# A wait for landed gathers in the middle of each group of the two max passes

## The reference

```
def _gin_layer(h, src, dst, W, b):
    msgs = h[src]
    agg = jax.ops.segment_max(msgs, dst, num_segments=N_NODES)
    agg = jnp.where(jnp.isfinite(agg), agg, jnp.zeros_like(agg))
    return (h + agg) @ W + b
x = _gin_layer(h, src, dst, W1, b1)
x = jax.nn.relu(x)
x = _gin_layer(x, src, dst, W2, b2)
```

## Time and profile before

| | |
|---|---|
| median of 3 timed runs | 5820.93 us (5820.36 to 5821.15) |
| span of the one profiled execution | 6562.2 us |
| POOL busy in that span | 3944.3 us, 60% |
| DVE busy | 4507.3 us, 69% |
| PE busy | 2310.6 us, 35% |

### The profile page before, as it was taken

The page is one execution under the profiler, slowest core; times in us unless marked ns, Lnnn a source line. Parts: engine busy times, 40 slices in busy tenths (PEclk is TensorE's granted clock), DMA queues, the critical chain, the costliest instruction groups (busy, mean ns, idle before and its releaser), DMA issues.

```text
span 6562.2 us, 44574 instructions
## 1 busy us (share of the span) xinstructions
PE 2310.6 (35%) x14635; PEld 1387.8 (21%) x14635; DVE 4507.3 (69%) x5353; ACT 2519.0 (38%) x3136; POOL 3944.3 (60%) x3878
## 2 busy tenths in 40 slices
PE   4988400000020000000100000046877783778886
PEld 2775300000000000000000000023444441444443
DVE  7978587777767777776787777764655653656654
ACT  2330144444424444443344444433444442444443
POOL 1001377777747777775677777656665555566664
PEclk8998755555555555555555555567888895889887
DMA  2233354444434444443454444412333322333332
GB/s 64 83 136 135 110 163 152 153 147 146 152 117 151 157 148 147 152 148 113 134 160 152 147 148 146 142 46 86 102 110 101 101 95 73 102 110 109 98 103 84
DMA packets 257146, 807.72 MB, mean 123 GB/s; under 512 B 72026, under 2 KB 108938, under 8 KB 253123
## 3 DMA queue, kind: packets, MB, share of 16 engines
q0 software_dynamic: 162688, 416.67, 22.2%
q1 hardware_dynamic: 94279, 389.14, 16.2%
HBM read 473.23 MB, written 332.30 MB: 123 GB/s over the span
## 4 chain that ended last, share of the span: by engine, by line
POOL 38%; PE 26%; issue 22%; DVE 8%; ACT 2%; another core or an unknown queue 2%; DMA 1%; SPq 0%; DVEq 0%; POOLq 0%; ACTq 0%
POOL arena L2316 38%; PE pair_ps L1864 20%; PE pair_ps L1966 3%; DVE outs L917 2%; ACT outs L1702 1%; PE banks_ps L1830 1%; PE banks_ps L1942 1%; DVE outs L995 1%; PE pair_ps L1873 0%; DVE bn_st L700 0%; DVE H L1048 0%; ACT arena L1680 0%; PE pair_ps L1982 0%; PE banks_ps L1807 0%
## 5 line engine op out<-in xcount | busy, mean ns | idle before, releaser
L2316 POOL DMA_INDIRECT arena<-table,src_i x3596 | 3684.6, 1025 | 1549.8 <-issue 1134.4
L1842 PE MATMUL pair_ps<-ident,tails 128*128 128x128 f32 x9 | 2.7, 439 | 3331.7 <-DVE tails L1246 3331.7
L1864 PE MATMUL pair_ps<-bias,arena 128*128 128x384 bf16 x4050 | 803.9, 348 | 279.9 <-issue 239.9
L1092 DVE TENSOR_TENSOR pair_ps<-pair_ps,arena 128x1792 f32<-128x1792 f32 x168 | 341.5, 2033 | 764.7 <-DMA arena<-table,src_i 589.1
L1864 PE MATMUL pair_ps<-work,arena 128*128 128x384 bf16 x4050 | 760.5, 338 | 206.4 <-issue 204.8
L995 DVE TENSOR_TENSOR_SCAN outs<-arena,banks_ps 128x1920 f32<-128x1920 f32 x112 | 465.2, 4153 | 494.3 <-ACT banks_ps L1688 446.2
L1842 PEld LDWEIGHTS pair_ps<-ident,tails 128*128 128x128 f32 x9 | 1.5, 213 | 3334.0 <-DVE tails L1246 3334.0
L1140 DVE TENSOR_TENSOR_SCAN work<-work,banks_ps 128x1920 f32<-128x1920 f32 x168 | 697.7, 4153 | 5.8
L1562 ACT ACTIVATE LD<-DE 128x112 f32<-128x112 f32 x168 | 49.8, 296 | 1440.9 <-issue 571.3
L1864 PEld LDWEIGHTS pair_ps<-bias,arena 128*128 128x128 bf16 x4050 | 406.9, 102 | 661.6 <-issue 452.8
L1582 ACT COPY outs<-work 128x1792 f32<-128x1792 f32 x171 | 541.0, 3165 | 0.0
(11 more groups left out here) (321 smaller groups left out, 4353.4 us busy)
## 6 DMA issues: line engine op xcount, KB each, us to landing
rows_att<-outs SPq DMA_DIRECT2D x165, 1008.0 KB
rows_plain<-outs SPq DMA_DIRECT2D x110, 896.0 KB
arena<-table,src_i POOLq DMA_INDIRECT x3596
kept_counts<-arena SPq DMA_DIRECT2D x15, 2000.0 KB, 6.4
bias<-sources SPq DMA_DIRECT2D x108, 192.0 KB
arena<-kept_counts SPq DMA_DIRECT2D x10, 2000.0 KB, 8.3
outs<-kept_counts SPq DMA_DIRECT2D x5, 2000.0 KB, 8.0
table<-arena SPq DMA_DIRECT2D x18, 512.0 KB, 3.0
```

The source lines that it names most:

```text
L1092: chain(v.tensor_tensor(prod, prod, ring[:, s, :, 0:D], ALU.mult))
L1864: ins = pe.matmul(picked_ps[g % 2], parts3[:, a, t, :], hots_made[g % 2][:, :, t, :], start=t == a == 0, stop=t == NB - 1 and a == 2)
L2316: pool.indirect_dma_start(dst, None, tab, bass.IndirectOffsetOnAxis(ap=idx, axis=0))\
```

## The change

In both max passes POOL gets one more wait in each group: after the first half of the group's gathers (7 of 14 in groups 0 and 1, 5 of 11 after them) it waits until all of that half have landed, and only then issues the second half. That is 56 waits in a pass and 112 in all. No instruction is moved, added or removed on the other engines, and the attention passes are as they were.

```diff
                         if g >= RING:
                             pool.wait_ge(s_spread, scanned(k, g - RING))
-                        for j in range(GROUP - picks(k, g)):
+                        n = GROUP - picks(k, g)
+                        for j in range(n):
+                            if j == n // 2:
+                                pool.wait_ge(s_land[g % RING], landed(k, g) - 16 * (n - j))
                             fetch(ring_plain[:, g % RING, j, :], table[k], src_i[:, g * GROUP + j:g * GROUP + j + 1],
                                   s_land[g % RING])
```

## The result

| | before | after |
|---|---|---|
| median of the timed runs | 5820.65 us (5817.55 to 5821.15, 4 runs) | 5992.16 us (5987.11 to 6000.26, 4 runs) |
| span of the recorded execution | 6562.2 us first, 5811.0 us when it was recorded again | 5992.8 us |
| idle time before the edge gathers (L2316, 3596 of them), ended by a gather's landing | none | 208.1 us |

The ratio is 1.0297 with a 95% interval of 1.0282 to 1.0311: 171.5 us slower, 171.5 / 112 = 1.53 us for each of the 112 waits. Forecast were 5980 us and 1.41 us.

The account below looks back on a forecast made before the run. POOL was taken to bound the timed max passes, 13.0 us a group against PE's 12.5; 112 waits x 1.41 us = 158 us on 5821 gave 5979, rounded to 5980 us, own range 5920 to 6045, overall range 5815 to 6100.

Parts of the forecast that it names:

- POOL ends last in the timed max passes: In the timed max passes POOL needs 13.0 us a group against PE's 12.5 us, so it has no slack.
- The split of the 741 us: Profiled execution's excess over the timed median: 403 us from PE's idle time in max passes, 338 us from 3745 gathers.
- The price of a wait: On POOL in the max passes: 2.60 us from gather to waiter's start, less 1.185 us, so 1.41 us a wait.
- two neighbours in the trace: Two trace places used to price a wait: ACT waiting for a group 0 gather, and POOL waiting for its own scatter.
- The scatter's 1.24 us: Where POOL waits for its own scatter to HBM, idle is 1.54 instead of 0.30 us; would make 139 us in all.
- All 112 waits count: In both max passes each wait passes straight to ACT, DVE's scan and the next slot: 112 x 1.41 = 158 us.
- The span: Profiled execution's span, 6562.2 us, would move by under 30 us, POOL's 3.6 us of slack a group covering the waits.
- The test I gave: If the recorded span moves as much as the timed median, both have the same bound and the 741 us reading is wrong.
- No change: Rival, chance 0.18: PE's idle time is in timed max passes too, waits vanish in the ring of slots; 5827 us.
- faster: Rival, chance 0.13: pauses in mid-group let PE run in the max passes, saving 146 us; 5675 us.
- PE's stall: In profiled max passes PE idles 1.6 to 2.3 us between matmuls of one group, without releaser; taken as absent when timed.
- Much slower: Rival, chance 0.09: in half the max-pass groups DVE's compares hold the gather after the pause, adding 308 us; 6287 us.

Follow-up runs that it names:

- four kernels of the table: Four edits of the kernel before: one wait mid-group (the change), after the 3rd gather (6013.7 us) or after the 7th (6039.2 us), and two waits a group (6311.4 us).
- The kernel with eight gathers: Kernel before with 8 gathers instead of 11 in each group from the third on: 5644.0 us; with the change's waits besides, 5653.3 us.
- the kernel with two waits: The change with two waits a group, after a third and two thirds of the gathers, instead of one in the middle: 6311.4 us, ratio 1.0836 to the kernel before.
- the late wait: The change with its one wait after the 7th gather of every group instead of the middle: 6039.2 us, ratio 1.0393 to the kernel before.

## Why the prediction was right

**POOL ends last in the timed max passes.** Right, and it carried the forecast. The profile that I had showed the opposite, 3.6 us of slack in every group. What turned it was the 741 us between the first recording and the median, and that PE's idle time had no releaser and stood inside a group. The second recording shows it: no such idle time, no slack of POOL. The margin over PE is larger than forecast, 14.0 against 12.5 us and not half a microsecond. Had I read the slack straight, I would have forecast no change.

**The split of the 741 us.** Half right. The prediction put 403 us of them in the max passes and took the other 338 us from the gap before every gather, so that a timed gather would come every 1.185 us and a group take 13.0 us. It comes every 1.27 us, and a group takes 14.0 us: the gap of 0.30 us before a gather is real. What was slow in the first recording's attention passes was the gathers themselves, 1056 ns; in the second:

```profile
L2316 POOL DMA_INDIRECT arena<-table,src_i x603 | 578.3, 959 | 183.7 <-issue 182.2 <-DVE pair_ps L1085 1.5
```

603 gathers in the 800 us that held 570. From the first edge gather to the last, the two max passes took 1004.0 and 993.1 us in the first recording and 790.2 and 790.1 us in the second, 417 us less, close to the 403 forecast; the three attention passes took 244.5 us less, and the rest of the 751 us between the two spans lies outside these passes. The wrong step was to spread the other 338 us over the gap before every gather. The error was harmless for the forecast, since both cadences leave POOL over PE's 12.5 us.

**The price of a wait.** Mis-sized by 0.12 us: 1.41 us forecast, 1.53 us timed, 1.55 us of idle time in the recording. All 112 idle stretches came, 1.86 us on average in place of the 1.6 us that I gave as a sign. Of the two neighbours in the trace the gather was the nearer one: 2.60 - 1.26 = 1.34 us, where POOL's own 2.81 us from a gather to its next start make 2.81 - 1.26 = 1.55 us. The scatter's 1.24 us was too low. The wrong cadence of 1.185 us had put 0.07 us on and so, by luck, hidden a third of the miss.

Luck had a larger part in the 2.60 us. They are of one gather of group 0. In the same first recording ACT started 2.53 us behind the last gather of group 1, but 4.48 us behind that of group 2 (4435.05 to 4439.53), and the prediction gives no reason why the 5th gather should land like the former. A wait of 4.48 - 1.26 = 3.2 us would have made some 6180 us. That the change's waits stand behind gathers that land in 2.8 us I hadn't argued.

By an estimate from the Trainium skill's fixed cost of about 2.0 us (DMA: Bandwidth & Descriptors, section Anatomy of one DMA — SWDGE (gpsimd) path) the time would have been 5912 us. The measured time is 5992 us: from the start of a gather to POOL's next start it was 2.8 us here.

**All 112 waits count.** Right. In all four kernels of the table the span grows by what POOL's gathers grew by. The kernel with eight gathers shows when they wouldn't count: with 2.3 us of slack a group the waits cost 9.3 us in all.

**The span.** Wrong as I put it. I expected it to move by under 30 us, because the first recording's slack would cover the waits. That stall didn't come back, so the span moved with the median: 181.8 us up from the second recording, 569.4 us down from the first. The test I gave, that span and median moving together would refute the reading of the 741 us, was badly made: it took for granted that every recording has the stall.

**The rivals.** No change and faster both needed PE's stall in the timed kernel; the second recording has none, and the changed kernel none either. Much slower, by gathers that DVE's compares hold, didn't come with the change: 108 of its 112 waits end outside the compares, and its gathers grew by 6.6 us in all. With two waits it came, at 117.8 us.

The Trainium skill's rule that GpSimd can't write descriptors while a DVE operation holds the shared port pair (SBUF — State Buffer, section SBUF: two separate sides) agrees with the 54 gathers of the kernel with two waits that ended 0.82 to 0.84 us behind the compares. With the late wait only 9 of 103 were held so: not every gather that starts among the compares is held to their end.

No version faster than the kernel before came of this. The experiments point to fewer gathers in a group, 14.0 us of POOL against 12.5 us of PE, but the steps taken off must be picked by PE, and three of them already take those 12.5 us; a finer split wasn't tried.

## What to carry to other kernels

Set the span of a recorded execution against the timed median before you read any slack from it; where the span is 13% longer, ask which idle time has no releaser, and what ends last without it. A wait for an engine's own transfer cost the landing less one issue interval here, on every pass through it, where that engine ended last, and next to nothing where the engine had to wait anyway. Take the landing from several places of the trace, and from the place where the wait will stand: here it ran from 2.4 to 5.8 us. Where another engine can hold the issuing one, it also matters what runs at the moment when the wait ends.

## What the runs showed of the hardware that was not expected

- The kernel before was recorded with spans of 6562.2 and 5811.0 us. In the slow recording PE stood for up to 2.3 us between matmuls while gathers streamed, and the attention passes' gathers took 1056 ns in place of 959 ns. What differs between the two recordings stays open.
- A semaphore wait that is already met in front of a gather costs nothing that can be measured: 110 of them, ratio 0.9993 (0.9984 to 1.0003).
- After a wait for a gather of 128 rows of 512 bytes POOL started again 2.81 us after the gather's start on average (2.66 to 3.90, 112 waits of the change), of which the gather's own instruction is 0.95 us. ACT, waiting for the last gather of a group in the second recording of the kernel before, started 2.44 to 5.76 us after that gather's start.
- A gather behind a wait that starts while the 15 compares run is either held to 0.82 to 0.84 us behind their end (54 of 98 with two waits a group, 9 of 103 with the late wait) or takes at most some 0.4 us longer than 0.95 us.
